# A fused attention and FFN layer: the residual kept transposed, the FFN result scattered into the output by DMA, and the 34 identity products taken out

## The chip, the cores and the metric

The kernel runs on one core of a Trainium2 chip. The metric is the device time of one execution in microseconds (us); the time before is the median of three runs. TensorE is PE in the profile, its weight loads PEld, VectorE DVE, ScalarE ACT, GpSimd POOL, and SyncE, which only issues DMAs here, SP.

## The reference, cut to what matters

x is 32 sequences of 32 tokens of width 512, all float32. Three steps follow each other:

```python
w = weights[subjects]                                  # 32x32 per sequence
c = einsum('bct,bcd->bdt', x, w)                       # conditioning
x = x + attn(c, wq, wk, wv, wo)                        # 32 heads of 16, rotary, causal, softmax
# second conditioning: base product plus two of eight experts of rank 16
base   = x @ W.T
logits = x @ Wr.T + 5.0 * one_hot(language)            # top 2 of 8, softmax -> gates
z = base + 2.0 * sum_e gates[e] * (x @ A[e].T) @ B[e].T
# FFN in 16 blocks: columns permuted, 32 -> 128 -> 32 in each block, permuted back
t = gelu(einsum('bhd,hdm->bhm', z[:, perm].reshape(-1, 16, 32), up))
x = x + einsum('bhm,hmd->bhd', t, down).reshape(-1, 512)[:, argsort(perm)]
```

The last line is what the change is about: the FFN's result stands in permuted columns, and has to come back to the columns of x before it is added.

## The kernel before, in words

The 1024 tokens go through in G = 4 groups of N = 256 tokens (two tiles, t = 0 and 1, of 128). Nearly every product of float32 data is made as three products of split numbers (`mm3`, lines 474 to 476): each operand is a high part, which ACT copies out (L818), and the low part left over, which DVE subtracts (L1011, from PSUM; L1018 for weights). So what a product waits for is nearly always a pair: an ACT copy, then a DVE subtraction.

Every engine runs a list written out by hand, and semaphores tie the lists together. PSUM has three rings of banks: A (2) for conditioning, Q, K and V; S (2) for scores and for the FFN's second product; F (4) for the rest. A product waits until the bank's last reader is done.

Per group g, in the program's names:

- `cond`: x times the block-diagonal `wbd` that `blocks` builds from the gathered 32x32 weights (L501). `blocks(0)` is DVE's, `blocks(1)` ACT's (L833), the later ones DVE's. The result, split, is `xc`.
- `qk`, `v`: Q, K, V of the next group, `xc` times the weights. `rope` (shuffle and product on DVE, L1059, L1061; product and sum on POOL, L412, L416) empties the banks of Q and K; a `rope` on DVE waits until POOL is done with the one before, since both use the buffer `rot`. V is copied out by ACT. `k_blocks` (L1081 on DVE, L427 on POOL) spreads K for the scores.
- `scores`, `max_shift`, `exp`, `sums`, `norm`, `turn`, `probs_block`: softmax, turned and spread into `pbd` by ACT in four copies of 32 partitions each (L818). `pv` (L566) multiplies by V.
- `o_out` (ACT) and `o_lo` (DVE) split the attention result into `attn`, which is the buffer `x1`. `wo_proj(g, t)` multiplies it by wo, tokens down the partitions: tile t needs only pv of tile t. `add_x` (L1119) adds it into `xs`, which holds x in rows of tokens. `turn_x1` (L587) transposes the sum, four products for each tile, and it is split again into `x1`.
- `lora_down`, `experts_base`, `turn_logits`, `gates_*`, `turn_gates`, `gate_h`, `experts_lora`: the second conditioning. `ffn_up`, `gelu` (ACT, L900), `ffn_down`: the FFN. These belong to group g - 1 and stand between the products of groups g and g + 1.
- `y_out` (ACT) and `y_lo` (DVE) split the FFN's result y. `unpermute` (L680) multiplies it by the 0/1 matrix `unperm`, 16 products of 512 columns for a group; it puts the columns back and turns the tokens down the partitions. `add_ffn` (L1196) adds it into `xs`, and SP stores `xs` as the output.

There are XS = 3 buffers of x. The x of group 3 takes the buffer of group 0, so its load waits for the store of group 0. Ahead of the first conditioning stand 20 products of the identity with itself, and 14 more between it and the first Q (`keep_busy`, L689); nothing reads their results.

At the start the conditioning weights of groups 1 to 3 go from HBM to SBUF (`cond_seqs`), back to HBM (`rows`), and into another shape (`wg`). ACT's list has `blocks(1)`, which waits for that, ahead of the high parts of wv. In group 0, DVE's list has the low parts of wo between the last `turn` and the third `rope` of group 1.

Of the kernel before, what the change touches and what calls it, by code (L numbers as in the profile page):

```python
# [18 lines left out]
F32 = mybir.dt.float32  # L19
# [8 lines left out]
P = 128  # L28
# [13 lines left out]
XS = 3  # L42
# [37 lines left out]
def build(nc, x, who, wcond, wq, wk, wv, wo, w2b, wr, wa, up, down, perm, consts, cols, rows, out):  # L80
    ctx = ExitStack()
    with ctx:
# [12 lines left out]
        unperm = sb("unperm", [P, KC, D], F32R)  # L95
# [18 lines left out]
        y2 = sb("y2", [P, 2, KC, N], F32R)  # L114
# [4 lines left out]
        permc = sb("permc", [P, KC], I32)  # L119
        upw = sb("upw", [P, KC, FM])  # L120
# [12 lines left out]
        raw_w2b = [xs[:, 2, :, :].rearrange("p c d -> p (c d)")[:, 0:WB]] + [kbd1[:, WB * c:WB * c + WB]  # L133
# [3 lines left out]
        col_no = act1[:, 0:D]  # L137
        raw_r = rows_of(act1[:, D:D + KC * E])

        attn = x1  # L140
        hg = y2[:, :, 0, :]
# [34 lines left out]
        permf = cut(KC)  # L176
# [34 lines left out]
        def f_ffn(g):  # L211

            f_fill((g, "XT", 1), (g, "LR"), (g, "LH"), (g, "W", 0), (g, "LT"), (g, "W", 1), (g, "GTR"))
            f_fill(*((g, "UP", r, j) for r in range(2) for j in range(4)))

        f_fill((0, "PV", 0), (0, "PV", 1), (0, "WO", 0), (0, "WO", 1), (0, "XT", 0))
        for _g in range(1, G - 1):
            f_ffn(_g - 1)
            f_fill((_g, "PV", 0), (_g, "PV", 1), (_g - 1, "UN", 0), (_g - 1, "UN", 1), (_g, "WO", 0),
                   (_g, "WO", 1), (_g, "XT", 0))  # L220
        f_ffn(G - 2)
        f_fill((G - 1, "WO", 0), (G - 2, "UN", 0), (G - 1, "XT", 0), (G - 2, "UN", 1), (G - 1, "WO", 1))
        f_ffn(G - 1)
        f_fill((G - 1, "UN", 0), (G - 1, "UN", 1))
# [46 lines left out]
        def wait_w(eng, name, n=2):  # L271

            eng.wait_ge(w_lo, W_AT[name] + n)
# [28 lines left out]
        d_wq2, d_cols = sem("d_wq2"), sem("d_cols")  # L302
        d_up, d_dn, d_wg, d_wgs = sem("d_up"), sem("d_dn"), sem("d_wg"), sem("d_wgs")
        w_hi, w_lo = sem("w_hi"), sem("w_lo")
# [6 lines left out]
        unperm_ready = sem("unperm_ready")  # L311
# [9 lines left out]
        x1_hi = sem("x1_hi")  # L321
# [3 lines left out]
        y_hi = sem("y_hi")  # L325

        x_d = x.rearrange("(g t b) c d -> g (b c) t d", g=G, t=GT)
        out_d = out.rearrange("(g t b) c d -> g (b c) t d", g=G, t=GT)
# [5 lines left out]
        def _(sp):  # L334
            def load_x(g):
                sp.dma_start(xs[:, g % XS, :, :], x_d[g]).then_inc(d_x[g], 16)

# [21 lines left out]
            sp.dma_start(dn[:, :, :], down).then_inc(d_dn, 16)  # L359
            wait_w(sp, "wv")  # L360
            sp.dma_start(col_no, cols).then_inc(d_cols, 16)
# [3 lines left out]
            load_x(2)  # L365
            for g in range(G):

                for t in range(GT):
                    wait_read(sp, Fi(g, "UN", t))
                    if g == G - 1:  # L370
                        sp.dma_start(out_d[g, :, t, :], xs[:, g % XS, t, :]).then_inc(d_out[g], 16)
                if g < G - 1:
                    sp.dma_start(out_d[g], xs[:, g % XS, :, :]).then_inc(d_out[g], 16)
                if g + XS < G:

                    sp.wait_ge(d_out[g], 16)
                    load_x(g + XS)
            for g in range(G):
                sp.wait_ge(d_out[g], 16 * GT if g == G - 1 else 16)
# [3 lines left out]
        def _(pool):  # L383
# [48 lines left out]

            def norm(g, i):
# [14 lines left out]
            wait_w(pool, "wq")  # L448
            pool.memset(pbd[:, 0, :, :, :], 0.0).then_inc(pbd_zero, 1)
            for i in range(3):  # L450
                rope(0, i)
            for t in range(GT):
                for c in range(2):
                    k_blocks(0, t, c)
            for g in range(G):
                norm(g, 0)
                norm(g, 1)
                if g + 1 < G:
# [3 lines left out]
                if g + 1 < G:  # L462
                    for i in range(1, 4):
                        rope(g + 1, i)
                    for t in range(GT):
                        k_blocks(g + 1, t, 1)
                        k_blocks(g + 1, t, 3)


        @block.tensor  # L470
        def _(pe):
# [100 lines left out]
            def wo_proj(g, t):  # L572
                it = Fi(g, "WO", t)
# [794 lines left out]
```

## Time and profile before

| | |
|---|---|
| median of 3 runs (lowest, highest) | 265.93 us (265.58, 266.53) |
| the profiled execution's own time | 266.65 us |
| its span, first to last instruction | 264.8 us |
| mean granted clock of TensorE | 0.955 |
| PE busy | 233.0 us, 88% of the span |
| PE weight loads | 194.6 us |
| DVE busy | 163.5 us |
| ACT busy | 118.4 us |
| POOL busy | 91.9 us |
| L680, unpermute, 64 products | 16.2 us in all, 403 ns for one |
| L689, identity products, 68 recorded rows | 9.9 us in all |
| L587, transposes of the sum, 32 recorded rows | 4.8 us in all |
| chain that ended last | PE 50%, DVE 19%, ACT 11%, DMA 10% |

Rows of PE overlap (one starts before the last has drained), so what a product costs the next one is the distance of two starts, not the duration of one. A row of a timeline gives start, length, engine, line, and in brackets how long the engine had stood idle and who released it.

### The profile page before, as it was taken

Reading aid. Unit: us, or ns where it says so; the run is one execution under the profiler, and the core shown is the slowest. Engines: PE = TensorE matmul, PEld = TensorE weight load, DVE = VectorE, ACT = ScalarE, POOL = GpSimd, SP = SyncE. Lnnn points to the kernel's source line nnn. Section 1 sums busy time; section 2 is a strip of 40 time slices with the busy share of each in tenths; the row PEclk is TensorE's granted clock in tenths of the full one; section 3 lists DMA queues with packets and bytes.
Section 4 is the critical chain, followed back from the end, with each engine's and each line's share of the span. In section 5 each row is a group of like instructions: output and inputs, shape, how many; then the busy total and the mean of one; then the engine's idle time right before and its main releaser. Section 6 shows DMA issues by size and latency. Waiting matters only on the chain.

```text
span 264.8 us, 5842 instructions
## 1 busy us (share of the span) xinstructions
PE 233.0 (88%) x2472; PEld 194.6 (73%) x2472; DVE 163.5 (62%) x328; ACT 118.4 (45%) x199; POOL 91.9 (35%) x76
## 2 busy tenths in 40 slices
PE   5999498997779999998989999989996888969775
PEld 5999376985558899876867999757685666739543
DVE  2651999999835778848437977484479704424313
ACT  3332456640603234868024248681324599203470
POOL 8259763384920016768000058590001400000000
PEclk9999899997979999999999999999999579979999
DMA  7698421000000000000220000000100000020002
GB/s 229 215 339 280 149 50 57 2 0 0 4 0 0 2 2 1 4 2 0 82 79 2 2 0 2 0 2 26 57 2 0 0 4 0 2 79 2 0 0 79
DMA packets 7529, 11.66 MB, mean 44 GB/s; under 512 B 2032, under 2 KB 2704, under 8 KB 7504
## 3 DMA queue, kind: packets, MB, share of 16 engines
q1 hardware_dynamic: 6784, 9.81, 10.8%
q0 software_dynamic: 432, 1.48, 1.7%
q8 instruction: 19, 0.31, 0.5%
q10 hardware_dynamic: 288, 0.01, 0.1%
q14 instruction: 6, 0.05, 0.1%
HBM read 9.07 MB, written 2.23 MB: 43 GB/s over the span
## 4 chain that ended last, share of the span: by engine, by line
PE 50%; DVE 19%; ACT 11%; DMA 10%; issue 7%; POOL 2%; DVEq 0%; ACTq 0%; SPq 0%; POOLq 0%
PE ps_F L474 7%; PE ps_F L476 7%; PE ps_F L475 6%; PE ps_F L680 6%; ACT pbd L818 5%; PE ps_A L474 5%; PE ps_A L476 4%; PE ps_A L475 4%; DMA rows<-kr 3%; PE ps_F L653 3%; ACT act L900 2%; DMA wg<-rows 2%; PE ps_S L548 2%; PE ps_F L566 2%; PE ps_A L501 1%
## 5 line engine op out<-in xcount | busy, mean ns | idle before, releaser
L436 POOL TENSOR_TENSOR pr<-pr,small 128x512 f32<-128x512 f32 x16 | 16.6, 1048 | 86.7 <-DVE small L1103 86.7
L818 ACT ACTIVATE pbd<-pr 32x512 f32<-32x512 f32 x64 | 40.2, 628 | 9.8 <-DVE pr L1109 5.0
L818 ACT ACTIVATE x<-ps_F 128x512 fp32r<-128x512 f32 (+1 forms) x22 | 13.1, 597 | 49.1 <-PE ps_F L587 35.5
L412 POOL TENSOR_TENSOR rot<-rot,cst 128x512 f32<-128x512 f32 x14 | 18.0, 1288 | 20.2 <-DVE rot L1059 20.2
L1081 DVE TENSOR_TENSOR kbd<-kr,cst 128x512 f32<-128x512 f32 x16 | 20.8, 1342 | 3.6 <-POOL kr L416 3.5
L427 POOL TENSOR_TENSOR kbd<-kr,cst 128x512 f32<-128x512 f32 x16 | 21.1, 1346 | 2.7 <-PE ps_F L483 2.6
L474 PE MATMUL ps_A<-wvT,xc 128*128 128x512 f32 x32 | 14.8, 464 | 5.8 <-DVE wvT L1018 3.5
L1011 DVE TENSOR_TENSOR y<-ps_S,y 128x512 fp32r<-128x512 f32 x8 | 5.5, 688 | 22.8 <-ACT y L818 22.7
L474 PE MATMUL ps_A<-xc,wqT 128*128 128x256 f32 x64 | 18.2, 284 | 1.3 <-DVE xc L1011 1.3
L474 PE MATMUL ps_A<-xc,wkT 128*128 128x256 f32 x64 | 18.3, 286 | 0.0
L474 PE MATMUL ps_F<-x,w2T 128*128 128x256 f32 x64 | 18.3, 286 | 0.0
L900 ACT ACTIVATE act<-ps_F 128x512 f32<-128x512 f32 x32 | 16.5, 604 | 3.4 <-PE ps_F L653 3.3
L476 PE MATMUL ps_A<-xc,wqT 128*128 128x256 f32 x64 | 17.9, 280 | 0.0
L475 PE MATMUL ps_A<-xc,wqT 128*128 128x256 f32 x64 | 17.9, 279 | 0.0
L475 PE MATMUL ps_A<-xc,wkT 128*128 128x256 f32 x64 | 17.9, 279 | 0.0
L476 PE MATMUL ps_A<-xc,wkT 128*128 128x256 f32 x64 | 17.8, 279 | 0.0
L475 PE MATMUL ps_F<-x,w2T 128*128 128x256 f32 x64 | 17.8, 279 | 0.0
L476 PE MATMUL ps_F<-x,w2T 128*128 128x256 f32 x64 | 17.8, 278 | 0.0
L1119 DVE TENSOR_TENSOR xs<-ps_F,xs 128x512 f32<-128x512 f32 x8 | 5.5, 692 | 19.3 <-PE ps_F L476 19.3
L474 PE MATMUL ps_F<-woT,x 128*128 128x512 f32 x32 | 13.5, 422 | 4.1 <-DVE x L1011 4.1
L680 PE MATMUL ps_F<-unperm,y 128*128 128x512 f32 x64 | 16.2, 403 | 0.1
L860 ACT ACTIVATE pr<-pr 128x512 f32<-128x512 f32 x16 | 10.0, 629 | 14.2 <-DVE pr L1095 14.1
(156 smaller groups left out, 643.8 us busy)
## 6 DMA issues: line engine op xcount, KB each, us to landing
xs<-in_x SPq DMA_DIRECT2D x4, 512.0 KB, 4.5
out<-xs SPq DMA_DIRECT2D x3, 512.0 KB, 2.8
pbd<-in_L_attn_wq SPq DMA_DIRECT2D x2, 512.0 KB, 5.2
act<-in_L_attn_wk SPq DMA_DIRECT2D x1, 1024.0 KB, 5.6
act<-in_L_attn_wv SPq DMA_DIRECT2D x1, 1024.0 KB, 8.6
act<-in_L_attn_wo SPq DMA_DIRECT2D x1, 1024.0 KB, 8.0
out<-xs SPq DMA_DIRECT2D x2, 256.0 KB, 2.0
x<-in_L_cond_A SPq DMA_DIRECT2D x1, 256.0 KB, 8.2
```

Of the source, the lines that this page charges most:

```text
L412: pool.tensor_tensor(rv, rv, con("sin").unsqueeze(1).to_broadcast([P, 2 * N // T, T]), ALU.mult).then_inc(rot_sin, 1)
L427: pool.tensor_tensor(kbd[:, t, c, :, :].rearrange("p b (h s) -> p b h s", h=HG), kv.unsqueeze(2).to_broadcast([P, BT, HG, T]), con("head") ...
L436: pool.tensor_tensor(pr[:, i, :, :], pr[:, i, :, :], mx[:, i, :].unsqueeze(2).to_broadcast([P, NH // 2, T]), ALU.mult).then_inc(normed, 1)
L474: pe.matmul(dst, hi_l, hi_r, start=start, stop=False, skip_group_check=skip)
L475: pe.matmul(dst, hi_l, lo_r, start=False, stop=False, skip_group_check=skip)
L476: return pe.matmul(dst, lo_l, hi_r, start=False, stop=stop, skip_group_check=skip)
L653: last = pe.matmul(bank(it)[:, N * (c % 2):N * (c % 2) + N], upw[at, c, :], x2[at, c, :], start=True, stop=True)
L680: last = pe.matmul(bank(it)[:, :], y2[:, part, c, P * t:P * t + P], unperm[:, c, :], start=(c == 0 and part == 0), stop=(c == KC - 1 and p ...
L818: return sc.activation(dst, src, ACT.Copy)
L860: sc.activation(pr[:, i, :, :], pr[:, i, :, :], ACT.Exp, scale=float(HD) ** -0.5).then_inc(exped, 1)
L900: sc.activation(act[:, r, j, :, :], bank(it)[:, :].rearrange("p (h n) -> p h n", h=2), ACT.Gelu).then_inc(s_free(it), 1)
L1081: ve.tensor_tensor(kbd[:, t, c, :, :].rearrange("p b (h s) -> p b h s", h=HG), kv.unsqueeze(2).to_broadcast([P, BT, HG, T]), con("head").u ...
```

## The change

1. The residual is kept transposed. A transposed copy of x, `xT`, is a new input (laid out outside the launch, as the weights are), loaded into `xt` (two buffers). `wo_proj(g, i)` now has the weights on the other side and gives channels down the partitions, so `add_x` adds into `xt`, and `x1_out`, `x1_lo` split that from SBUF. `turn_x1` is gone. Each `wo_proj` now needs the attention result of both tiles. `lora_down` takes its operands in halves.
2. The FFN's result is not multiplied by `unperm`. SP stores `xt` as the output right after `add_x`; later POOL adds each 128 rows of y (1 KB each, straight copies of PSUM by ACT, no split) to the output rows named by `row_at`, with four indirect accumulating DMAs for each group. The output is transposed in HBM, and turned back outside the launch. `unpermute`, `y_lo`, `add_ffn` and `unperm` are gone.
3. `keep_busy` is gone.
4. The attention result is split into `xc` in place of `x1`, so `o_out` waits for V of the next group, which reads `xc`.
5. Lists: ACT makes the high parts of wv ahead of `blocks(1)`, and those of wo ahead of the first V. POOL makes the low parts of wo in place of DVE, after its first two `norm`, and clears `pbd` after the first `k_blocks` rather than before `rope`. DVE has `rope(1, 2)` and `rope(1, 3)` right after the last `turn` of group 0. In the last group all of `pv` stands ahead of the last two `ffn_down`, and those ahead of `wo_proj`.
6. x has two buffers, and its loads wait for `cond` alone; the output's store no longer stands ahead of one.

```diff
-XS = 3
+XS = 2
...
+            wait_full(sp, A(0, COND + 1))
+            load_x(2)
+            load_xt(0)
...
+                sp.dma_start(out_d[g], xt[:, g % 2, :, :]).then_inc(d_x1[g], 16)
+                if g + 2 < G:
+
+                    sp.wait_ge(d_x1[g], 16)
+                    sp.wait_ge(x1_low, 2 * g + 2)
+                    load_xt(g + 2)
...
+            def add_rows(g):
+
+                pool.wait_ge(rows_ready, G)
+                pool.wait_ge(d_x1[g], 16)
+                for c in range(KC):
+                    wait_read(pool, S_down(g, c // 2))
+                    pool.indirect_dma_start(out=out, out_offset=bass.IndirectOffsetOnAxis(
+                                                ap=row_at[:, g, c:c + 1], axis=0),
+                                            in_=y[:, c, :], in_offset=None, compute_op=ALU.add
+                                            ).then_inc(d_out[g], 16)
...
+            def wo_proj(g, i):
+                it = Fi(g, "WO", i)
                 wait_free(pe, it)
                 for t in range(GT):
+                    wait_read(pe, PVi(g, t))
+                W, o = WT["wo"], attn
+                for h in range(2):
+                    c = 2 * i + h
+                    for k in range(KC):
+                        last = mm3(bank(it)[:, N * h:N * h + N],
+                                   W[:, 0, k, P * c:P * c + P], W[:, 1, k, P * c:P * c + P],
+                                   o[:, 0, k, :], o[:, 1, k, :], k == 0, k == KC - 1)
                 last.then_inc(s_full(it), 1)
...
-            keep_busy(20)
             cond(0, 0)
             cond(0, 1)
-            keep_busy(14)
...
             def y_out(g, i):
...
+                if g:
+                    sc.wait_ge(d_out[g - 1], 16 * KC)
+                copy(y[:, 2 * i:2 * i + 2, :], bank(it)[:, :].rearrange("p (c n) -> p c n", n=N)
+                     ).then_inc(s_free(it), 1)
...
+            def add_x(g, i):
+                it = Fi(g, "WO", i)
+                half = xt[:, g % 2, 2 * i:2 * i + 2, :]
                 wait_full(ve, it)
+                ve.wait_ge(d_xt[g], 16)
+                ve.tensor_tensor(half, bank(it)[:, :].rearrange("p (c n) -> p c n", n=N), half, ALU.add
                                  ).then_inc(s_free(it), 1)
```

Three places show what moves in the lists. The first is ACT near the start; `wvT` are the high parts of wv, `wbd` is `blocks(1)`, `vz` the copy of the first V. Before:

```order
L818 ACTIVATE wkT<-act 128x1024 x2
L833 ACTIVATE wbd<-wg,cst 128x2x32 x4
L818 ACTIVATE wvT<-act 128x1024 x2
L818 ACTIVATE w2T<-ps_F 128x512 x3
L818 ACTIVATE bT<-ps_F 128x512
L818 ACTIVATE vz<-ps_A 128x16x2x16
L818 ACTIVATE woT<-act 128x1024 x2
```

Now:

```order
L802 ACTIVATE wkT<-act 128x1024 x2
L802 ACTIVATE wvT<-act 128x1024 x2
L817 ACTIVATE wbd<-wg,cst 128x2x32 x4
L802 ACTIVATE w2T<-ps_F 128x512 x3
L802 ACTIVATE bT<-ps_F 128x512
L802 ACTIVATE woT<-act 128x1024 x2
L802 ACTIVATE vz<-ps_A 128x16x2x16
```

wv has changed places with `wbd`, and wo with the first V. The second place is DVE in group 0, from the last two `turn` (L1109, now L1096) on. Before:

```order
L1109 STREAM_TRANSPOSE pr<-pr 128x512 x2
L1018 TENSOR_TENSOR woT<-act,woT 128x1024 x2
L1043 TENSOR_SCALAR wbd<-wg,cst 128x2x32 x4
L1059 STREAM_SHUFFLE rot<-ps_A 128x512
L1061 TENSOR_TENSOR kr<-ps_A,cst 128x512
L1018 TENSOR_TENSOR aT<-x,aT 128x512
L1018 TENSOR_TENSOR rT<-act,rT 128x32
L1030 TENSOR_SCALAR unperm<-act,small 128x512 x4
L1059 STREAM_SHUFFLE rot<-ps_A 128x512
L1061 TENSOR_TENSOR kr<-ps_A,cst 128x512
L1081 TENSOR_TENSOR kbd<-kr,cst 128x512 x4
L1011 TENSOR_TENSOR x<-ps_F,x 128x4x128 x2
```

Now:

```order
L1096 STREAM_TRANSPOSE pr<-pr 128x512 x2
L1046 STREAM_SHUFFLE rot<-ps_A 128x512
L1048 TENSOR_TENSOR kr<-ps_A,cst 128x512
L1030 TENSOR_SCALAR wbd<-wg,cst 128x2x32 x4
L1046 STREAM_SHUFFLE rot<-ps_A 128x512
L1048 TENSOR_TENSOR kr<-ps_A,cst 128x512
L1005 TENSOR_TENSOR xc<-ps_F,xc 128x4x128
L1068 TENSOR_TENSOR kbd<-kr,cst 128x512 x2
L1005 TENSOR_TENSOR xc<-ps_F,xc 128x4x128
L1068 TENSOR_TENSOR kbd<-kr,cst 128x512 x2
L1012 TENSOR_TENSOR aT<-x,aT 128x512
```

The two `rope` have come up, the low parts of wo and `unperm` have left the list, and the attention result (`xc<-ps_F`, before `x<-ps_F`) stands among the `k_blocks`. The third place is PE in the last group, from the FFN's first product of group 2 (L653, now L676) on. Before (the list goes on with a `wo_proj` between the sixth row and the seventh):

```order
L653 MATMUL ps_F<-x,upw 128x256 x8
L566 MATMUL ps_A<-pbd,vz 32x128 x16
L653 MATMUL ps_F<-x,upw 128x256 x8
L665 MATMUL ps_S<-act,dn 32x256 x8
L566 MATMUL ps_A<-pbd,vz 32x128 x16
L665 MATMUL ps_S<-act,dn 32x256 x8
...
L566 MATMUL ps_A<-pbd,vz 32x128 x16
L680 MATMUL ps_F<-unperm,y 128x512 x8
L587 MATMUL ps_F<-cst,xs 128x128 x4
L566 MATMUL ps_A<-pbd,vz 32x128 x16
L680 MATMUL ps_F<-unperm,y 128x512 x8
```

Now:

```order
L676 MATMUL ps_F<-x,upw 128x256 x8
L596 MATMUL ps_A<-pbd,vz 32x128 x16
L676 MATMUL ps_F<-x,upw 128x256 x8
L688 MATMUL ps_S<-act,dn 32x256 x8
L596 MATMUL ps_A<-pbd,vz 32x128 x48
L688 MATMUL ps_S<-act,dn 32x256 x8
L504 MATMUL ps_F<-xc,woT 128x256
```

All the `pv` of the group (L566, now L596) now stand ahead of the first product with wo, which before followed when half of them were done.

## Rows read from the trace of the kernel before

**Rows 1.** Waits of PE: who released it, us in total, times, the longest

```profile
PE ps_F L474 <- DVE x L1011: 5.6, 3, 3.4
PE ps_A L474 <- DVE wvT L1018: 3.5, 1, 3.5
PE ps_A L474 <- DVE kr L1061: 2.4, 1, 2.4
PE ps_F L587 <- DVE xs L1119: 1.3, 2, 0.9
PE ps_A L501 <- DMA xs<-in_x: 1.3, 1, 1.3
```

**Rows 2.** Timeline of PE at the start: start, length, line, count, idle before

```profile
2.96 6.58 PE L689 MATMUL ps_S<-cst 128*128 128x128 f32 x40 [2.96 <-DMA cst<-constants]
9.58 2.02 PE L501 MATMUL ps_A<-wbd,xs 128*128 128x128 f32 x16
```

**Rows 3.** Timelines of DVE and ACT, 8 to 32 us

```profile
8.70 0.74 DVE L1043 TENSOR_SCALAR wbd<-wg,cst 128x64 f32<-128x64 f32 x4 [0.83 <-DMA wg<-in_L_cond_weights,idx]
...
31.13 0.73 DVE L1059 STREAM_SHUFFLE x<-ps_A 128x512 f32<-128x512 f32 x1
...
24.53 1.07 ACT L833 ACTIVATE wbd<-wg,cst 128x64 f32<-128x64 f32 x4 [8.25 <-DMA wg<-rows]
```

**Rows 4.** Timelines of DVE and POOL in group 0

```profile
55.87 3.78 DVE L1018 TENSOR_TENSOR woT<-act,woT 128x1024 fp32r<-128x1024 f32 x2
...
56.40 2.16 POOL L416 TENSOR_TENSOR qr<-qr,rot 128x512 f32<-128x512 f32 x1
```

**Rows 5.** Timeline of PE at the end of group 0

```profile
74.54 0.47 PE L474 MATMUL ps_F<-woT,x 128*128 128x512 f32 x1 [3.39 <-DVE x L1011]
...
82.20 1.95 PE L501 MATMUL ps_A<-wbd,xs 128*128 128x128 f32 x16
```

**Rows 6.** Five stretches: length, busy of PE, PEld, DVE, ACT, POOL, PEclk, DMA

```profile
74.54:81.77 7.23, 7.23 (x25) 5.67 (x25) 1.14 (x2) 0.00 (x0) 0.15 (x1) 0.76 0.00 0
128.84:134.45 5.61, 5.61 (x26) 4.47 (x25) 1.38 (x2) 0.00 (x0) 0.00 (x0) 1.00 0.32 117
122.83:126.95 4.12, 2.96 (x41) 2.43 (x41) 3.18 (x4) 2.19 (x4) 2.19 (x2) 1.00 0.00 0
217.53:220.44 2.91, 1.07 (x16) 0.53 (x17) 1.34 (x3) 2.60 (x6) 0.00 (x0) 1.00 0.00 0
232.86:235.87 3.01, 0.63 (x5) 0.45 (x6) 1.38 (x2) 0.60 (x1) 0.00 (x0) 0.95 0.10 35
```

**Rows 7.** Timelines of PE and DVE at the end of group 1

```profile
125.01 4.00 PE L680 MATMUL ps_F<-unperm,y 128*128 128x512 f32 x16
...
126.26 0.69 DVE L1011 TENSOR_TENSOR x<-ps_F,x 128x512 fp32r<-128x512 f32 x1 [0.94 <-ACT x L818]
```

**Rows 8.** Timelines of ACT and PE in the last group

```profile
220.38 5.13 ACT L818 ACTIVATE pbd<-pr 32x512 f32<-32x512 f32 x8
...
235.87 0.37 PE L474 MATMUL ps_F<-x,rT 128*8 128x256 f32 x1 [1.50 <-DVE x L1011]
```

**Rows 9.** ACT's last two copies of y; POOL's gathers into kbd (ns min/median/max, starts)

```profile
256.12 0.63 ACT L818 ACTIVATE y<-ps_S 128x512 fp32r<-128x512 f32 x1
257.53 0.60 ACT L818 ACTIVATE y<-ps_S 128x512 fp32r<-128x512 f32 x1 [0.78 <-PE ps_S L665]
...
L403 POOL DMA_INDIRECT kbd<-in_w2b,permc x3: 942/942/1110, 16.3 to 19.0; - x3
```

**Rows 10.** DMA issues: queue, count, KB each, median us from issue to landing

```profile
out<-xs SPq DMA_DIRECT2D x2, 256.0 KB, 2.0
...
act<-in_L_attn_wv SPq DMA_DIRECT2D x1, 1024.0 KB, 8.6
...
rows<-kr SPq DMA_DIRECT2D x1, 128.0 KB, 9.2
...
kbd<-in_w2b,permc POOLq DMA_INDIRECT x3, 5.0
```

More of the change, by code:

```diff
@@ L77, in constants, with build @@
     return c
-def build(nc, x, who, wcond, wq, wk, wv, wo, w2b, wr, wa, up, down, perm, consts, cols, rows, out):
+def build(nc, x, xT, who, wcond, wq, wk, wv, wo, w2b, wr, wa, up, down, perm, consts, rows, out):
     ctx = ExitStack()
@@ L582, in turn_x1 @@
[L582 to L587 removed]
+                for h in range(2):
+                    c = 2 * i + h
[3 more added lines that the diff above has]
+                                   o[:, 0, k, :], o[:, 1, k, :], k == 0, k == KC - 1)
@@ L716, in _ @@
                         cond(g + 1, 1)
-                    turn_x1(g - 1, 1)
                     scores(g, 0)
@@ L777, in _ @@
                 wo_proj(g, 0)
-                if not more:
-                    pv(g, 1, 0)
-                    pv(g, 1, 1)
-                    unpermute(g - 1, 0)
-                    turn_x1(g, 0)
-                    pv(g, 1, 2)
-                    pv(g, 1, 3)
-                    unpermute(g - 1, 1)
                 wo_proj(g, 1)
-                if more:
-                    turn_x1(g, 0)
                 if g == 0:
@@ L808, in _ @@
                 ffn_down(G - 1, c)
-            for half in range(2):
-                for t in range(GT):
-                    unpermute(G - 1, t, (half,))
         @block.scalar
@@ L965, in _ @@
                     y_out(g - 1, 0)
-                if more:
-                    probs_block(g, 1, 0)
-                o_out(g, 0)
-                if more:
+                probs_block(g, 1, 0)
+                if more and g:
+                    o_out(g, 0)
                     v_out(g + 1, 0)
-                if g:
                     y_out(g - 1, 1)
-                if not more:
-                    probs_block(g, 1, 0)
+                elif more:
+                    v_out(g + 1, 0)
+                    o_out(g, 0)
+                else:
+                    o_out(g, 0)
                 probs_block(g, 1, 1)
@@ L977, in _ @@
                     v_out(g + 1, 1)
-                else:
-                    x1_out(g, 0)
                 o_out(g, 1)
-                if more:
-                    x1_out(g, 0)
-            x1_out(G - 1, 1)
+                if not more:
+                    y_out(g - 1, 1)
+                x1_out(g, 0)
+                x1_out(g, 1)
             h_out(G - 1)
```

249 lines of the change are left out of this document (100 added, 149 removed).

## The prediction, made before the changed kernel ran

> **What bounds the kernel now.** I read the page's busy shares first, then who waits for whom, then the timelines around each wait of PE. PE is busy 88% of the span, and half of the chain that ended last is PE's, so a product that goes is a gain unless something was running under it. PE stands idle in few places, and the list of its waits names them [rows 1]: 5.6 us before products with wo (3.4 at the longest), 3.5 before the first V, 2.4 before the second, 1.3 for the load of x, 1.3 before the transposes. Each long one costs twice: after it the granted clock falls to 1.2 GHz for a while. The stretch from 74.54 to 81.77, the two `wo_proj` of group 0 after a 3.39 us wait, took 7.23 us at a mean grant of 0.76; the same 24 products from 128.84 on took 5.61 at 1.00 [rows 5, 6]. So one fall costs 1.6 us, and a warm product of 256 columns about 0.117 (5.61 / 24 / 2).
>
> All sums below are in the trace's own times: span 264.8, own time 266.65.
>
> **The start: 3.9 us less.** The 20 identity products end at 9.54, and `wbd`, without which no conditioning can run, is complete on DVE at 9.44 [rows 2, 3]. So their removal moves nothing forward there. It leaves PE cold: conditioning (2.0 us warm) takes perhaps 1.2 more, then come the copy and the subtraction (0.6 and 0.7), and Q begins near 13.9, about where the 14 other products let it begin now. Q and K are 96 products, 11.2 us warm, plus 1.6 for the clock: K is complete near 26.8.
>
> What follows was held by wv, not by PE. ACT's list has `blocks(1)` ahead of wv, and that waited until 24.53 for the weights' round trip through HBM [rows 3]; wv itself had landed near 17.7 (issued as the first gather was in, at about 9, and 8.6 us on the way [rows 10]). With the order changed the low parts of wv fit on DVE among the first `rope`, and the last `rope` (31.13 now) begins when K and DVE are ready, near 27.2. That is 3.9 us; POOL's `rope` and `k_blocks` come forward as well, since the clearing of `pbd` has moved behind them. If the clock stayed low through all of Q and K, 96 times 0.1 or 9 us would be added in place of 1.6, and all of this term would be lost and 4 us more.
>
> **The rest of group 0: 7.6 us less.** DVE spends 3.78 us from 55.87 on with wo, and the `rope` that empties K's bank stands behind it [rows 4]. Now it comes first. It must wait for POOL's `rope(1, 1)`, done at 58.56 now [rows 4], earlier by the 3.9 of the start and by nearly another 0.9 if DVE no longer reads two SBUF operands beside it. That is about when K's products end, so the 2.4 us wait before V goes, and with it one fall of the clock, 1.6. On POOL the low parts of wo are two operations of 1024 columns, so four times a 512-column one: 8.6 us at the 2.16 that one took beside DVE's wo [rows 4], about 5 if DVE leaves it alone, which I take; there they lie in a gap of 6 us before `rope(1, 0)`. Without that gap they would delay `rope` by their length.
>
> The 3.4 us wait before `wo_proj` and its fall, 1.6, go too: the attention result no longer stands behind six other DVE items. But `wo_proj` now needs both tiles, so after the last `pv` PE waits for a copy and a subtraction, about 1.4. In all 2.4 + 1.6 + 3.4 + 1.6 - 1.4 = 7.6.
>
> The Trainium skill (SBUF — State Buffer, Who interferes with whom) says that a VectorE instruction with two SBUF inputs contends with a GpSimd instruction that reads SBUF. By it POOL's new wo work would slow only DVE operations of that kind, and in that gap DVE mostly reads PSUM; the sum would stay as it is.
>
> **Products that go.** Before the last group's scores six `turn_x1` of 0.43 each (81.77 to 82.20, [rows 5, 6]) go: 2.6. `unpermute` is 4.0 us for a group [rows 7], but it ran while the second tile's attention result was being split: that subtraction ends at 126.95, and `wo_proj` now begins there instead of at 128.84 [rows 6, 7]. So a removal of 4.0 gives 1.9, twice (group 2 repeats the pattern): 3.8. The 1.3 us wait for x goes, since its buffer is free when conditioning has read it [rows 1]. With 0.4 of the waits before the transposes, the share of group 2: 2.6 + 3.8 + 1.3 + 0.4 = 8.1.
>
> **The last group: 2.4 us less.** ACT's eight copies into `pbd` run from 220.38 to 225.51 now [rows 8]. `y_out(2, 1)` now stands behind them and `o_out` between them, so they end near 224.7; then `pv` 1.1, `ffn_down` 1.1 beside the split (1.4): `wo_proj` begins at 227.1. PE stood idle some 6 us by then in two pieces, so I charge a fall: 5.6 + 1.6, end at 234.3. The first half of `lora_down` runs while the second half of the sum is added and split (2.2 us), the second half takes 12 * 0.117 = 1.4 from 236.5: done at 237.9. Before, its 24 products began at 235.87 with the clock down [rows 8]: 235.87 + 2.8 + 1.6 = 240.3. The gate chain behind is unchanged.
>
> **The end: 0.8 us more.** The two copies of y end at 256.75 and 258.13 [rows 9]. From there the old kernel needs 6.7 us (subtraction, `unpermute`, add, store). Now POOL starts four issues one after the other; the gathers into `kbd` start about 1.3 apart and take 1 us each [rows 9]. The fourth begins at 256.8 + 3 * 1.3 = 260.7. No row shows an accumulating transfer. The nearest are the gathers of 128 rows, 5.0 us from issue to landing; below lies the plain store of 256 KB, 2.0, above the slowest transfer of 128 KB, 9.2 [rows 10]. I take 4.9: it ends at 265.6. The bounds are 262.7 and 269.9, or -2.1 and +5.1. In groups 0 to 2 the adds have tens of us.
>
> The Trainium skill (DMA: Bandwidth & Descriptors, Anatomy of one DMA) fits a transfer from GpSimd by 2.0 us and its bytes over 436 GB/s, an estimate of 2.3 us for 128 KB. By that the end would be 2.6 us earlier, and the forecast 243.7.
>
> **The clock at the new waits: 1.6 us more.** Before `wo_proj` of groups 1 and 2 PE will stand idle twice, 1.2 us (as at 122.83 now) and 1.9, with 1.1 us of `pv` between: two pieces of wait close together. In 232.86 to 235.87, 0.63 busy of 3.01, the clock fell; in 217.53 to 220.44, 1.07 busy of 2.91, it did not [rows 6]. I take one fall of the two, 1.6; none and two are the bounds.
>
> **The sum.** -3.9 - 7.6 - 8.1 - 2.4 + 0.8 + 1.6 = -19.6. From the profiled 266.65 that is 247.05; the median lies 0.7 under the profiled run, so **246.3 us**.
>
> **Rivals.**
>
> - *Clock.* The clock falls in both groups, or comes up late after the cold start: for it speaks that all fillers are gone, against it that Q and K are 11 us of unbroken work. +1.6 to +7: 248 to 253. The Trainium skill (TensorE: Matmul & The Clock Gate, HAM oscillation) describes a kernel in which a wait in every tile drops the clock in every tile; by that both groups would fall, 247.9. I give this 0.22.
> - *The start does not move.* Wo, x and xT share the DMA queues near 23 us; if wo landed late, ACT, which waits for it ahead of the first V, would hold the softmax. Or POOL's wo work delays `rope`. Up to 5 us back: 250 to 252. 0.13.
> - *No falls and fast adds.* -1.6 and -2.1: 242.6 to 244. The plain store speaks for it. 0.15.
> - *Slower than before.* The accumulating DMAs read and write HBM row by row, and four may follow each other rather than overlap. One after the other at X us each, the tail is 4X against 8 now. The rest of the sum is worth 20.4 us, so from X of about 7 it decides: at the 9.2 of the slowest transfer it is 36.8 - 8 - 20.4, or 8 us slower, 274. Against it: the gathers of `kbd` overlapped. 0.04.
> - *My likeliest case* has 0.46, 245 to 248.
>
> **Range and chances.** 243.0 to 251.0: from no falls and fast adds to both falls with a lost start term; about 2 in 10 lie outside. Faster by over 0.3% (about what a measurement of this kernel can tell from no change): 0.95; within it 0.01, the edge of the last rival; slower 0.04.
>
> **What the new profile would show.** No wait of PE before the second V, and V of group 0 right behind the transposes of w2, with the first `max_shift` near 33 (start term). PE idle about 1.4 us before `wo_proj` of group 0, 1.9 in groups 1 and 2, with PEclk at 1.00 or not through it. Conditioning of group 2 near 70 (82.20 now), the last group's first scores near 170 (190 now). Four accumulating DMAs in a row at the end, the last landing 5 us after its issue. The prediction is wrong if the adds take 9 us, if PEclk stays at 0.5 beyond 18 us, or if a wait for POOL's wo shows before `wo_proj`.

## The result and the profile after

The changed kernel takes 252.83 us (median of 4 runs, 251.96 to 253.62) against 265.75 for the kernel before in the same session (4 runs, 264.51 to 266.53): a ratio of 0.9517, interval 0.9467 to 0.9567. It is faster, as forecast, but by 13 us and not by 19.6: 246.3 was predicted, and 252.83 lies above the range's upper end of 251.0. Times are medians over all executions; the ratios leave out those that took over 1.5% longer than the fastest of the same kernel.

The page of the changed kernel: span, busy times, then tenths in 40 slices, and the chain that ended last.

```profile
span 250.2 us, 5702 instructions
...
PE 205.5 (82%) x2404; PEld 176.3 (70%) x2404; DVE 147.8 (59%) x309; ACT 119.0 (48%) x199; POOL 120.0 (48%) x94
...
PE   0579997999699999995999999949994828987910
...
PEclk9999999999999999998899999998998895999995
...
PE 60%; DVE 14%; ACT 12%; issue 7%; POOL 2%; DMA 2%; POOLq 1%; ACTq 0%; DVEq 0%
```

PE lost 27.5 us of work and the span only 14.6. The last two slices of PE are nearly empty: the end now belongs to POOL and DMA. The list of PE's waits, which answers to [rows 1]:

```profile
...
PE ps_A L596 <- ACT pbd L802: 6.5, 4, 4.2
PE ps_F L504 <- DVE xc L1005: 6.1, 3, 2.0
PE ps_F L504 <- DVE hg L1178: 4.5, 2, 3.2
PE ps_A L504 <- DVE xc L1005: 2.7, 2, 1.5
PE ps_F L596 <- ACT pbd L802: 2.3, 2, 1.2
```

The waits before V, for x and before the transposes are gone, as forecast. Before `wo_proj` (L504 with `xc`) PE now waits three times 2.02 us. What that does to the clock is in the windows, columns as in [rows 6]: the `wo_proj` of groups 0, 1, 2 and 3.

```profile
66.57:72.29 5.72, 5.72 (x48) 5.72 (x49) 3.77 (x6) 0.63 (x1) 0.53 (x1) 1.00 0.01 3
116.66:123.92 7.26, 7.26 (x48) 7.26 (x49) 1.39 (x2) 0.63 (x1) 3.13 (x3) 0.76 0.49 54
168.03:175.24 7.21, 7.21 (x48) 7.17 (x49) 1.38 (x2) 0.63 (x1) 3.13 (x2) 0.77 0.51 57
212.73:218.25 5.52, 5.52 (x49) 5.50 (x49) 1.38 (x2) 1.22 (x2) 3.14 (x2) 1.00 0.34 37
```

During `wo_proj` the clock was down in groups 1 and 2 and, in this execution, in neither of the others. The end, on ACT (copies of y) and POOL (the adding DMAs), answers to [rows 9]; the last line is from the list of DMA issues, as in [rows 10].

```profile
238.04 0.63 ACT L802 ACTIVATE y<-ps_S 128x512 f32<-128x512 f32 x1
239.45 0.60 ACT L802 ACTIVATE y<-ps_S 128x512 f32<-128x512 f32 x1 [0.78 <-PE ps_S L688]
...
239.60 1.56 POOL L453 DMA_INDIRECT out<-y,row_at  x1 [22.56 <-ACT y L802]
241.47 1.56 POOL L453 DMA_INDIRECT out<-y,row_at  x1 [0.30 <-issue]
243.33 1.56 POOL L453 DMA_INDIRECT out<-y,row_at  x1 [0.30 <-issue]
245.19 1.56 POOL L453 DMA_INDIRECT out<-y,row_at  x1 [0.30 <-issue]
...
out<-y,row_at POOLq DMA_INDIRECT x16, 3.8
```

The first issue comes 0.93 us after the first copy's end, the next three 1.86 apart, and the span ends 5.0 after the fourth begins. Set against the same places of the kernel before, stretch by stretch:

| stretch, up to | predicted | measured |
|---|---|---|
| end of DVE's first `k_blocks` (36.52, now 33.80) | -3.9 | -2.7 |
| conditioning of group 2 (82.20, now 72.29) | -8.0 (7.6 and one `turn_x1`) | -7.2 |
| first scores of the last group (190.17, now 175.24) | -6.1 (products -7.7, clock +1.6) | -5.0 |
| the last group's first product with w2 (240.07, now 222.00) | -2.4 | -3.1 |
| end of the span | +0.8 | +3.5 |
| sum (rounded after adding) | -19.6 | -14.6 |

The other 1.6 us lie between profiled run and median: I took 0.7 off, and this profiled run is 0.87 under its median. The four runs, in order of time, have mean clocks of 0.952 (251.96), 0.942, 0.938 and 0.932 (253.62).

### The profile page after: what moved, and what is told of

Read it like the earlier page. It is cut to its first block, busy times and chain, and to the rows that moved or that the text cites. A ratio compares the mean times of both kernels' runs of the same rounds, so it can differ in the third digit from the quotient of the medians.

```text
span 250.2 us, 5702 instructions
## 1 busy us (share of the span) xinstructions
PE 205.5 (82%) x2404; PEld 176.3 (70%) x2404; DVE 147.8 (59%) x309; ACT 119.0 (48%) x199; POOL 120.0 (48%) x94
## 4 chain that ended last, share of the span: by engine, by line
PE 60%; DVE 14%; ACT 12%; issue 7%; POOL 2%; DMA 2%; POOLq 1%; ACTq 0%; DVEq 0%
PE ps_F L504 8%; PE ps_A L504 8%; PE ps_F L506 7%; PE ps_F L505 7%; PE ps_A L506 7%; PE ps_A L505 7%; ACT pbd L802 7%; PE ps_F L596 3%; PE ps_F L676 3%; PE ps_A L531 3%; PE ps_S L578 2%; ACT act L884 2%; POOL out L453 2%; ACT xc L802 2%; DVE xc L1005 2%
## 5 line engine op out<-in xcount | busy, mean ns | idle before, releaser
L453 POOL DMA_INDIRECT out<-y,row_at x16 | 25.1, 1571 | 39.8 <-ACT y L802 36.1
L504 PE MATMUL ps_F<-xc,woT 128*128 128x256 f32 x64 | 19.7, 307 | 6.1 <-DVE xc L1005 6.1
L1068 DVE TENSOR_TENSOR kbd<-kr,cst 128x512 f32<-128x512 f32 x16 | 19.9, 1280 | 2.4 <-POOL kr L422 2.4
L504 PE MATMUL ps_A<-xc,wqT 128*128 128x256 f32 x64 | 18.9, 296 | 2.7 <-DVE xc L1005 2.7
L505 PE MATMUL ps_F<-xc,woT 128*128 128x256 f32 x64 | 19.2, 300 | 0.0
L506 PE MATMUL ps_F<-xc,woT 128*128 128x256 f32 x64 | 19.1, 299 | 0.0
L802 ACT ACTIVATE x<-xt 128x512 fp32r<-128x512 f32 x8 | 5.0, 631 | 28.9 <-DVE xt L1108 28.9
L504 PEld LDWEIGHTS ps_F<-xc,woT 128*128 128x128 f32 x64 | 13.5, 212 | 7.5 <-issue 7.5
L506 PE MATMUL ps_A<-xc,wqT 128*128 128x256 f32 x64 | 18.6, 290 | 0.0
L505 PE MATMUL ps_A<-xc,wqT 128*128 128x256 f32 x64 | 18.5, 289 | 0.0
L504 PE MATMUL ps_A<-xc,wkT 128*128 128x256 f32 x64 | 18.3, 286 | 0.0
L504 PE MATMUL ps_F<-x,w2T 128*128 128x256 f32 x64 | 18.3, 286 | 0.0
L531 PE MATMUL ps_A<-wbd,xs 128*128 128x128 f32 x64 | 9.7, 315 | 9.1 <-DVE wbd L1030 9.1
```

Source lines behind the costliest of these rows:

```text
L453: pool.indirect_dma_start(out=out, out_offset=bass.IndirectOffsetOnAxis(ap=row_at[:, g, c:c + 1], axis=0), in_=y[:, c, :], in_offset=None, ...
L504: pe.matmul(dst, hi_l, hi_r, start=start, stop=False, skip_group_check=skip)
L505: pe.matmul(dst, hi_l, lo_r, start=False, stop=False, skip_group_check=skip)
L506: return pe.matmul(dst, lo_l, hi_r, start=False, stop=stop, skip_group_check=skip)
L531: last = pe.matmul(bank(it)[:, P * c:P * c + P], xs[:, g % XS, t, P * c:P * c + P], wbd[:, t, :, :], start=True, stop=True)
L802: return sc.activation(dst, src, ACT.Copy)
```

## The experiments

The theories on the miss: (a) the identity products at the start are worth nothing; (b) the new waits before `wo_proj` cost a fall of the clock each time; (c) the order of wv and wo on ACT, DVE and POOL carries the gain of start and group 0; (d) the rest of the miss is the accumulating DMA. Each run's rival is in its expectation. Sessions differ by up to 1% in the time of the kernel before, so kernels of different sessions are compared by their ratios to it. Four of the runs were measured in one session: the products back, the filler before `wo_proj`, wv in its old place and the last group by PE. In it the kernel before itself ranged from 263.98 to 270.80 us, and the intervals of their ratios are 0.0115 to 0.0144 wide; two ratios that differ by less than that are not told apart by time alone.

**The products back.** The changed kernel with the 20 and 14 products where they were.

```diff
+            keep_busy(20)
             cond(0, 0)
             cond(0, 1)
+            keep_busy(14)
```

> The changed kernel with the 20 and the 14 identity products back at the start. Theory 1, the cold start is what the start term lacks: in the changed kernel conditioning took 3.75 us and the 48 products of Q 7.41 us, where warm products would take 2.0 and 5.9. With the products back K is complete about 1.5 us sooner, and the run is 1 to 1.5 us shorter than the changed kernel's 252.8, so 251.3 to 251.8. Theory 2, the start is held by the low parts of wv on DVE beside POOL's rope (1.98 and 2.33 us each): within 0.5 us of 252.8.

253.23 us (251.66 to 255.28), ratio 0.9507, interval 0.9435 to 0.9579: the same within the intervals. DVE near the first maximum, in this kernel and then in the changed one:

```profile
27.00 0.74 DVE L1053 STREAM_SHUFFLE x<-ps_A 128x512 f32<-128x512 f32 x1
...
30.64 2.86 DVE L1075 TENSOR_TENSOR kbd<-kr,cst 128x512 f32<-128x512 f32 x2
...
34.10 0.69 DVE L1087 TENSOR_REDUCE small<-ps_S 128x16 f32<-128x512 f32 x1
```

```profile
22.99 1.98 DVE L1012 TENSOR_TENSOR wvT<-act,wvT 128x1024 fp32r<-128x1024 f32 x1
...
26.14 2.33 DVE L1012 TENSOR_TENSOR wvT<-act,wvT 128x1024 fp32r<-128x1024 f32 x1
...
28.39 0.74 DVE L1046 STREAM_SHUFFLE x<-ps_A 128x512 f32<-128x512 f32 x1
...
34.39 0.69 DVE L1080 TENSOR_REDUCE small<-ps_S 128x16 f32<-128x512 f32 x1
```

With the products the last `rope` starts 1.39 us earlier, but POOL's `k_blocks` do not (30.14 to 32.96 here, 29.69 to 32.65 in the changed kernel); DVE's now run beside them and take 2.86 in place of 2.01, and the scores wait 0.90 us for POOL's. The first maximum comes only 0.29 earlier. A warm PE at the start gains nothing that is kept.

Other kernels here show the same without any products. In five of those below (scatter without addition, wo on DVE, the last group by PE, and two of those built on it) Q ran at full pace from its first product, and the last `rope` began between 26.4 and 27.3. The first maximum still came at 33.5 to 34.4, since POOL's `k_blocks` began at 29.5 to 29.8 in all five. POOL's timeline in the kernel with wo on DVE:

```profile
19.53 1.31 POOL L418 TENSOR_TENSOR rot<-rot,cst 128x512 f32<-128x512 f32 x1
...
29.49 2.82 POOL L433 TENSOR_TENSOR kbd<-kr,cst 128x512 f32<-128x512 f32 x2
```

From 19.5 on POOL is busy with `rope` nearly without a break. With wv in its new place the start is thus bound by when POOL begins its `rope`: 19.1 to 19.9 in these five, 21.75 in the kernel before, where the clearing of `pbd` (1.83 us) stood ahead of it. No run puts the clearing back, so its share is read from the traces and not shown by an experiment.

**No products in the kernel before.** The same from the other side: the kernel before without both `keep_busy`.

> The kernel before with its 34 identity products taken out, and nothing else changed. Theory 1, they are worth nothing there, since V waits for wv until 31 us, 5 us after K is complete: the same as before within 0.7 us. Theory 2, the cold start delays Q and K and through DVE's rope everything: 1 to 1.5 us slower.

265.92 us (12 runs) against 266.18 (17 runs): the medians are 0.1% apart. The ratio of 0.9959 (0.9923 to 0.9995) rests on 8 of the 12, so its small distance from 1 is no proof of a cost. The products are worth nothing there either.

**A filler before `wo_proj`.** Eight identity products, into a free bank, in the 2.0 us wait of groups 1 and 2.

```diff
                     ffn_down(g - 1, 3)
+                if 0 < g < G - 1:
+                    wait_read(pe, S_down(g - 1, 1))
+                    keep_busy(8)
                 wo_proj(g, 0)
```

> The changed kernel with 8 identity products (1.7 us at full clock) in the 2.02 us wait before the products with wo of groups 1 and 2. Theory 1, the wait makes the clock fall, which costs 1.6 us in each of the two groups: these stretches go from 7.26 and 7.21 us back to about 5.6, PEclk 1.00, and the run is 3.2 us shorter, 249.6. Theory 2, the clock falls for the earlier wait of 1.16 us or for the low activity as a whole, and 8 products don't hold it: 252.3 to 253.3.

250.56 us (249.55 to 252.36), ratio 0.9415, interval 0.9353 to 0.9477. Its windows over `wo_proj` of groups 1, 2 and 3:

```profile
116.90:122.60 5.70, 5.69 (x48) 5.70 (x49) 1.39 (x2) 0.63 (x1) 3.14 (x3) 1.00 0.64 69
167.00:172.80 5.80, 5.80 (x49) 5.76 (x50) 1.38 (x2) 0.63 (x1) 3.13 (x2) 1.00 0.62 68
210.70:217.40 6.70, 6.70 (x53) 6.67 (x50) 1.39 (x2) 1.23 (x2) 3.14 (x2) 0.85 0.38 42
```

Both stretches are back at full clock, 1.5 us shorter each. In the last group, which has no filler, `wo_proj` took 6.7 at 0.85; that is not the filler's doing, since this stretch varied between 5.5 and 6.8 us in the six kernels without any fillers. Theory (b) holds for groups 1 and 2: filling the wait of 2.02 is enough, though the 1.16 us wait ahead of `pv` stays. By time, the run is 2.7 us below the one with the products back, of the same session. Over all the kernels run here the pattern is sharp: in groups 1 and 2, without filler, 12 stretches of 12 ran slow (7.0 to 8.1 us from the first product to the next stage), and with filler 10 of 10 ran in 5.5 to 5.8. In group 0, after the same 2.0 us wait, the clock fell in 4 of 7 profiled kernels without filler there.

**wv in its old place.** ACT makes the high parts of wv behind `blocks(1)` again.

```diff
-            w_his("wv", raw["wv"], WT["wv"], (d_w["wv"], None))
             blocks(1)
+            w_his("wv", raw["wv"], WT["wv"], (d_w["wv"], None))
```

> The changed kernel with ACT's blocks(1) again ahead of the high parts of wv, one line moved. Theory 1, this order is what the start gained by: the first maximum of the scores goes from 34.4 us back to 36 to 37, and the run gets 2 to 3 us longer, 254.8 to 255.8. Theory 2, the start came forward for other reasons (the clearing of pbd moved on POOL, the wo order): within 0.7 us of 252.8.

254.94 us (254.37 to 256.04), ratio 0.9568, interval 0.9498 to 0.9638; 1.7 us above the run with the products back, of the same session. ACT's row that wv stood behind, and DVE's first maximum, 1.1 us later than in the changed kernel:

```profile
22.55 1.06 ACT L817 ACTIVATE wbd<-wg,cst 128x64 f32<-128x64 f32 x4 [6.22 <-DMA wg<-rows]
```

```profile
35.50 0.69 DVE L1080 TENSOR_REDUCE small<-ps_S 128x16 f32<-128x512 f32 x1
```

The profile gives the order of wv 1.1 us; the ratio's 1.4 us lie inside the uncertainty of both intervals. It is a part of the start's 2.7, and its size is smaller than theory (c) had it. Two rows show what else had moved: `blocks(1)` began at 22.55 and not at 24.53 as in [rows 3], so wv behind it came 2.0 earlier as well, and POOL began its `rope` at 20.07 and not at 21.75. The copy to `rows` landed after 8.3 us in this run, 7.2 in the changed kernel and 9.2 before [rows 10]; what made it faster no run isolates.

**wo on DVE again.** `wo_los` leaves POOL's list, and DVE makes the low parts of wo ahead of the third `rope`, as before.

```diff
                 norm(g, 1)
-                if g == 0:
-                    wo_los()
...
                 if g == 0:
+                    for h in range(2):
...
+                        ve.tensor_tensor(WT["wo"][:, 1, rows, :], raw["wo"][:, rows, :],
+                                         WT["wo"][:, 0, rows, :].bitcast(F32), ALU.subtract).then_inc(wo_lo, 1)
                     rope(1, 2)
```

> The changed kernel with one part undone: the low parts of wo are made on DVE again, between the last turn and the third rope of group 1 (3.8 us), not on POOL. Theory 1 (the prediction's second term is right: DVE's work with wo was what the V of group 1 waited for): PE waits about 2.4 us before V of group 1 again, conditioning of group 2 begins 2.5 to 4 us later than the 72.3 of the changed kernel, and the median is 255 to 257. Theory 2 (the V did not depend on it, since the rope there waits for POOL until 55.1 in any case, and the gain of group 0 came from the order of the attention result alone): V waits under 0.5 us longer, conditioning of group 2 begins within 1 us of 72.3, and the median is 252 to 254.

255.04 us (253.22 to 256.86), ratio 0.9557, interval 0.9498 to 0.9616. Timelines of DVE and PE in this kernel:

```profile
52.81 3.77 DVE L1259 TENSOR_TENSOR woT<-act,woT 128x1024 fp32r<-128x1024 f32 x2
56.51 0.71 DVE L1044 STREAM_SHUFFLE rot<-ps_A 128x512 f32<-128x512 f32 x1
```

```profile
57.85 0.50 PE L502 MATMUL ps_A<-wvT,xc 128*128 128x512 f32 x1 [1.62 <-DVE kr L1046]
```

The wait before V is back, 1.62 us, and conditioning of group 2 begins at 75.2 and not at 72.29: 2.9 later. Of that 1.5 is a fall of the clock in `wo_proj` of group 0, which other kernels had there without this edit (4 of 7, above), so 1.4 is what the edit shows. By the ratios the loss is 0.4%, inside both intervals. In the changed kernel the same `rope` began at 55.10, after 1.86 us of waiting for POOL, so moving 3.77 us off DVE moved it by only 1.4.

**Scatter without addition.** The expectation says what the output leaves out. One execution.

```diff
-                                            in_=y[:, c, :], in_offset=None, compute_op=ALU.add
+                                            in_=y[:, c, :], in_offset=None
```

> The changed kernel with the 16 scatters as plain writes, without the addition (the output then holds the FFN's result alone, x and attention are left out of it). Theory 1, a scatter of 128 rows costs POOL 1.56 us because it accumulates: without it an issue takes about 1.0 us, as the gathers do, the starts of the last four are 1.3 us apart in place of 1.86, and the end is 1.7 us shorter. Theory 2, it is the scatter itself (the indexed side is the written one, rows of 1 KB): issue 1.5 to 1.6 us and the end unchanged within 0.3 us; then only the landing could differ.

253.08 us, span 251.3. POOL at the end, and the list of issues:

```profile
243.82 0.97 POOL L453 DMA_INDIRECT out<-y,row_at  x1 [24.14 <-ACT y L802]
245.10 0.97 POOL L453 DMA_INDIRECT out<-y,row_at  x1 [0.30 <-issue]
246.38 0.97 POOL L453 DMA_INDIRECT out<-y,row_at  x1 [0.31 <-issue]
247.65 0.97 POOL L453 DMA_INDIRECT out<-y,row_at  x1 [0.30 <-issue]
...
out<-y,row_at POOLq DMA_INDIRECT x16, 2.4
```

The addition makes one issue 1.56 us in place of 0.97, the distance of two 1.86 in place of 1.28, and the median landing 3.8 in place of 2.4. From the end of the first copy of y (243.02) the end takes 8.3 us against 11.5: 3.2 us is what the addition costs there; the expectation had 1.7 from the distance of the issues alone, and the rest is mostly the landing. The whole did not get shorter, because ACT's second copy of V waited 3.16 us in group 1 and 3.02 in group 2 (1.20 in the changed kernel), for an event that the trace only calls remote. `wo_proj` then began after 3.98 and 3.84 us of waiting, with a deeper fall (7.5 us at 0.71, 8.1 at 0.67). What that event is stays open.

**The last group by PE.** y of group 3 is split and multiplied by a 0/1 matrix (32 products), DVE adds it into `xt`, and SP stores that; groups 0 to 2 scatter as in the change. The core of the edit:

```diff
-            add_rows(G - 1)
...
+            for i in range(2):
+                wait_read(pe, S_down(G - 1, i))
+                for t in range(2):
...
+                                last = pe.matmul(bank(it)[:, N * h:N * h + N], unperm[:, c, at:at + P],
+                                                 y2[:, part, c, :], start=(h == 0 and c == 0 and part == 0),
...
+                ve.tensor_tensor(half, bank(it)[:, :].rearrange("p (c n) -> p c n", n=N), half, ALU.add
```

> The changed kernel with the last group's result brought back by 32 products with the 0/1 matrix (built by DVE in its idle time of the last group, into the place of wq) and added into xt on DVE, stored by SP in halves; groups 0 to 2 still go by the accumulating DMAs. Theory 1, the four accumulating DMAs at the end cost 11.5 us from the last-but-one copy of y where the old end took 8.1: the end is 3.5 to 4.8 us shorter, 248.0 to 249.3. Theory 2, the end of the new kernel is bound by the store or by the matrix not being ready, or the extra DVE work delays the last wo products: 251 or more.

249.90 us (248.51 to 250.90), ratio 0.9378, interval 0.9320 to 0.9435. Its end, all engines:

```profile
239.58 0.60 ACT L832 ACTIVATE wkT<-ps_S 128x512 fp32r<-128x512 f32 x1
...
241.63 4.09 PE L821 MATMUL ps_F<-wkT,wqT 128*128 128x256 f32 x32
...
245.59 1.27 SPq L396 DMA_DIRECT2D out<-xt  x2
```

From the end of the first copy (240.18) to the end of the span are 8.9 us, against 11.5 with the four adding DMAs: 2.6 us less. The clock had fallen here in the last 32 products with `dn`; in the next kernel, with the same end and no fall there, it is 8.3 from the same point. The windows over those products, here and in the next kernel:

```profile
237.87:241.71 3.84, 3.60 (x34) 1.26 (x33) 0.69 (x1) 2.31 (x5) 0.00 (x0) 0.56 0.00 0
```

```profile
233.38:236.35 2.97, 2.14 (x33) 0.91 (x32) 0.69 (x1) 2.25 (x5) 0.00 (x0) 1.00 0.00 0
```

So theory (d) holds for the end: the last group's result costs 3.2 us more by adding DMAs than by products (11.5 against 8.3; 8.1 in the kernel before). By the ratios the run is 1.4% (3.7 us) below the changed kernel, where 3.5 to 4.8 were expected. In groups 0 to 2 no wait of PE or ACT in the changed kernel's profile is put down to the scatter; that it is free there is read from this and not tested by itself.

**Both together, with more fillers.** The kernel above with 8 products before `wo_proj` of groups 0 to 2, and 13 and 4 in the waits of `pv` in the last group; `fill(n, bank)` is n identity products.

```diff
+                if more:
+                    fill(8, Fi(g, "WO", 0))
                 wo_proj(g, 0)
...
+                    fill(13, Fi(g, "WO", 0))
                     for c in range(KC):
                         pv(g, 1, c)
+                        if c == 1:
+                            fill(4, Fi(g, "WO", 0))
```

> The changed kernel with the last group's result brought back on PE as in the run before, and identity products in the waits for the attention result: 8 before the wo products of groups 0, 1 and 2, and in the last group 13 and 4 in the waits for pbd. Theory 1, the clock falls for these waits, in group 0 in some executions only: all four stretches of wo run at PEclk 1.00, 5.6 to 5.8 us each, and the gains of the fills (2.3 us by the run with 8 in groups 1 and 2, and up to 3 more for groups 0 and 3) and of the end (2.9) add up: 244 to 247, with a narrower spread than the 1.7 us of the changed kernel. Theory 2, the falls come anyway at another place, or the fills delay pv in the last group: 248 or more.

245.33 us (245.05 to 245.89, 6 runs), ratio 0.9221, interval 0.9181 to 0.9262. The spread over the runs is 0.8 us, where it was 1.7 to 3.6 in the kernels without all of these fillers; in the three that follow, with more fillers still, it is 1.5 to 1.7.

**The gate waits.** Then 13 more in the last group's wait ahead of the gated product of group 2, and on top of that 14, and last 5, in the 1.3 us wait ahead of the gated product of group 3.

```diff
+                if g == G - 1:
+                    fill(13, S_down(g - 1, 0))
                 if g:
                     experts_lora(g - 1, 0)
...
             turn_gates(G - 1)
+            fill(5, S_down(G - 1, 0))
             experts_lora(G - 1, 0)
```

> The kernel with fills and the end on PE, with 13 more identity products in the 3.2 us wait for the gates in the last group, after which the changed kernel ran at half clock through the next 10 us. Theory 1, this stretch is on the path: from the gates to the first GELU of group 2, products and copies come 1.5 to 2.5 us sooner, and the run is that much shorter than the one without. Theory 2, ACT's chain (gelu and the copies into pbd) bounds the stretch and hides the clock: within 0.7 us of the one without.

> The kernel with the last group added by PE products and identity products in the waits before wo_proj, in the last group and ahead of the gates, plus 14 identity products in the 1.3 us wait for the gated product at the very end (group 3). Theory 1 (each product at half speed in the last stretch goes back to a wait close ahead of it): the products act,dn of group 3, which ran at half speed in the last stretch (3.8 us for 32), run at full speed in 2.2 us, and the median is 243.5 to 244.5. Theory 2 (that fall comes from the state of the chip at the time and not from this wait, or the wait that the products fill is on the chain and they lengthen it): the median stays at 245.0 to 246.0.

> As the kernel with 14 identity products in the last 1.3 us gate wait (e11_fill_last_gate, group 3), with 5 of them: the 14 took 3.1 us and held the gated product 1.6 us back, 5 take 1.1 us and fit into the wait. Theory 1 (the fall of the clock in the last 32 products act,dn goes back to that wait, and only the length of the filler was wrong): act,dn of group 3 keep full speed (2.2 us for 32), the gated product begins about 1.7 us after the transposes of the gates as in the kernel without filler there, and the median is 244.0 to 245.0. Theory 2 (no gain from this wait): the median stays at 245.0 to 245.8.

They took 245.21 (ratio 0.9215, 0.9172 to 0.9257), 246.07 (0.9237, 0.9191 to 0.9283) and 244.23 us (243.59 to 245.32; 0.9175, 0.9130 to 0.9220). In its profile the first gained 1.1 us up to `wo_proj` of the last group and lost 0.6 of it at the very end, where the clock fell as it had with the last group by PE; by time it is the same as the kernel without. (Its expectation speaks of half clock through 10 us; in the changed kernel it is 0.68 over the 5.4 us from 190.91 on, 1.00 over the next 4.6, and 0.53 from 206.1 to 212.7.) The windows over the last 32 products with `dn`, with 13 and then with 14 more:

```profile
232.20:236.03 3.83, 3.60 (x34) 1.25 (x33) 0.69 (x1) 2.31 (x5) 0.00 (x0) 0.55 0.02 4
```

```profile
233.58:236.55 2.97, 2.14 (x33) 0.92 (x32) 0.69 (x1) 2.25 (x5) 0.00 (x0) 1.00 0.00 0
```

With the 14 the clock was full there, but they took 3.1 us (0.22 each) in a wait of 1.3, and held the gated product up by 1.6: that was my error of size. Five fit, and the median is the 244.0 to 245.0 expected. That these fillers hold the clock at the end is likely and not shown: without them it fell there in 2 of the 9 profiled kernels that have the new attention part, and the intervals of these last ratios overlap. The page of that kernel has the clock full in every slice, and PE at 89%:

```profile
PE 216.7 (89%) x2554; PEld 187.7 (77%) x2554; DVE 152.1 (63%) x318; ACT 119.0 (49%) x199; POOL 113.9 (47%) x90
...
PEclk9999999999999999999999999999999999999999
```

It has the lowest median, 8.25% under the kernel before and 3.6% under the changed kernel by the ratios.

## Why the prediction was right in direction and too low

- *The start, -3.9 against -2.7.* Right: the products gave nothing, as the run that put them back shows. Wrong: the path. The term went by DVE's last `rope`, and with that early the first maximum was held by POOL's `rope` and `k_blocks`, at 33.5 to 34.4 in every such kernel. In this profile the `rope` was late too: K was complete at 27.4 (26.8 expected), but the last `rope` began at 28.39 and not at 27.2, because the low parts of wv took 1.98 and 2.33 us on DVE while POOL was busy beside it; the first of them took 1.35 in the run with the products, the second 2.13; over all the kernels they took 1.21 to 2.33. That "the low parts of wv fit on DVE among the first `rope`" was too kind.
- *The rest of group 0, -7.6.* Measured 0.8 short. The V wait went and POOL's work with wo (4.80 us, 5 expected) lay in its gap: the run with wo on DVE brought the wait back (1.62 us). The wait before `wo_proj` was 2.02 and not "about 1.4".
- *Products that go, -8.1.* With two falls priced at 1.6 each, the stretch up to the last group's scores has -8.2 for the 7.7 that was due there. This term stands, including the 1.9 for each 4.0 us `unpermute`.
- *The clock, "I take one fall of the two".* This step failed: both groups fell, in every profiled kernel without filler. It cost 1.6, and filling both waits gave back 1.0% (2.7 us) by the ratios, give or take 0.8%, where 3.2 was the price of two falls and 3.0 is what the windows show. I had one row for and one against, and split the difference; the pair of waits was the same in both groups, so half was the least likely outcome. The rule of the Trainium skill (TensorE: Matmul & The Clock Gate, HAM oscillation) that I had as a rival, a fall in every tile that has the wait, is what the traces show in groups 1 and 2; group 0, where it fell in 4 of 7, is not that regular.
- *The last group, -2.4 against -3.1.* I charged a fall to `wo_proj`. In the profiled run it came earlier, in the `pv` that wait for ACT (0.53 from 206.1 to 212.7), and was over when `wo_proj` began (5.52 at 1.00). In the other profiled kernels without filler there `wo_proj` took up to 6.8 us, so the charge is right for some executions, and it is a part of the 1.6 us between profiled run and median.
- *The end, +0.8 against +3.5.* This term was mis-sized most. The landing was right (5.0, 4.9 taken). The distance of the issues, "about 1.3 apart" from the gathers, is 1.86 with addition, 1.7 us over three; the start of the first issue 0.93 behind the copy, which I had at nothing, is the rest. Plain scatters are indeed 1.28 apart, so the row of the gathers was right for the DMA and wrong for the addition. By the Trainium skill's fit (DMA: Bandwidth & Descriptors, Anatomy of one DMA) 128 KB are an estimate of 2.3 us, near the plain scatter's median of 2.4 and far from the 3.8 of the adding one.

The misses by place: 2.0 in start and group 0, 1.6 clock, 2.7 end, 1.6 in the step from profiled run to median, less 1.3 that came out better: together 6.6, against the 6.5 between 246.3 and 252.8. What the 1.6 us of the last step consist of is open; the falls that come in some executions only are one part that the traces show.

The range was narrower than its own bounds. The end at its bound of +5.1 in place of +0.8 and both falls give 252.2, beyond the 251.0 that was stated. The rival with both falls had 248 to 253 at 0.22; its condition came true, and that 252.8 lies in it is luck, since the clock is 1.6 of the 6.5.

## What to carry to other kernels

Price a DMA that accumulates by its own row, and if there is none, assume that it both issues and lands slower than a plain one; in the middle of a kernel tens of us can cover it, while in the last group every microsecond of it is the end. When a transfer or an order is moved, look at every engine that feeds the next product: here DVE came early and POOL did not. When an edit creates the same wait in each stage, expect the clock to do the same in each stage, and test it with a filler cut to the wait: here 8 products of 0.22 us in a wait of 2.0 us gave 1.5 back, and 14 in a wait of 1.3 held the chain up by 1.6. Look at the later waits in more than one profile before a fall there is put down to the filler: both places where the clock fell behind one here had falls without it too.

## What the runs showed of the hardware that was not expected

- An accumulating indirect DMA of 128 rows of 1 KB: 1.56 us of POOL for an issue, 1.86 from one to the next, 3.8 to landing; without addition 0.97, 1.28 and 2.4.
- At the start PE is slow while the granted clock reads full. The 16 products of the first conditioning took 3.75 us from 9.10 (2.02 in [rows 2], behind the identity products), and 3.7 to 3.8 in all eleven kernels that begin without such products. Q behind it varies: in the changed kernel and three others its products are 0.21 us apart at first (here until 17.6 us) and 0.117 later, in the other seven 0.11 to 0.12 from the first. What decides it is open. This window of the changed kernel covers Q, at a grant of 1.00:

```profile
14.31:21.72 7.41, 7.41 (x50) 7.41 (x51) 3.67 (x5) 3.78 (x6) 5.83 (x6) 1.00 1.05 355
```

- The same wait of 2.02 us is followed by a fall in some executions and not in others (group 0: 4 of 7). The four runs of the changed kernel lie in the order of their mean clocks, 1.7 us for 0.020.
